# A perceiver block: places of the squares, a queue for the slots, a new layout of the preparation

## What is computed

```python
def _L0_xattn_ref(slots, P, Wq, Wk, Wv, gru_wih, gru_whh, gru_bih, gru_bhh, slot_norm_w, input_norm_w):
    ...
    Pn = rmsnorm(P, input_norm_w)
    k_proj = Pn @ Wk.T
    v_proj = Pn @ Wv.T
    for _ in range(NUM_ITERS):   # 3
        sn = rmsnorm(slots, slot_norm_w)
        q_proj = sn @ Wq.T
        scores = jnp.einsum('bkd,bmd->bkm', q_proj, k_proj) * SCALE
        attn = jax.nn.softmax(scores, axis=-2)
        attn = attn / (jnp.sum(attn, axis=-1, keepdims=True) + EPS)
        updates = jnp.einsum('bkm,bmd->bkd', attn, v_proj)
        slots = gru_cell(updates, slots, gru_wih, gru_whh, gru_bih, gru_bhh)
    return slots
...
x = x + _L0_xattn_ref(_layernorm(x, axis=-1), ctx_1024, ...)
x = x + _L0_attn_ref(...)
x = x + _L0_ffn_ref(...)
```

## Time and profile before

| | us |
|---|---|
| median of 3 runs | 1109.31 (1107.12 to 1110.37) |
| the profiled execution, its own time | 1099.15 |
| its span | 1097.4 |
| preparation, up to round 1 | 158.26 |
| rounds 1 to 12 | about 614 |

### The profile page before, as it was taken

The page is one execution under the profiler, slowest core; times in us unless marked ns, Lnnn a source line. Parts: engine busy times, 40 slices in busy tenths (PEclk is TensorE's granted clock), DMA queues, the critical chain, the costliest instruction groups (busy, mean ns, idle before and its releaser), DMA issues. The chain is left out here.

```text
span 1097.4 us, 38085 instructions
## 1 busy us (share of the span) xinstructions
PE 885.4 (81%) x17686; PEld 714.7 (65%) x17686; DVE 652.7 (59%) x1288; ACT 359.8 (33%) x651; POOL 4.6 (0%) x24
## 2 busy tenths in 40 slices
PE   3587567896988886988886899776597867999998
PEld 1444567886987886988886889776455744344443
DVE  3574537783884783874883876543624856345453
ACT  2552623333333333323333321110235623433321
POOL 0000000000000000000000000000000000000000
PEclk9788888998998998988998999897797987899999
DMA  9563970056173055253074250503123001322201
GB/s 336 220 178 72 221 147 3 4 85 174 22 113 129 3 97 162 33 105 125 5 114 144 47 128 33 117 3 117 40 46 80 21 20 54 101 94 94 99 19 38
DMA packets 159014, 99.97 MB, mean 91 GB/s; under 512 B 129740, under 2 KB 142084, under 8 KB 155788
## 3 DMA queue, kind: packets, MB, share of 16 engines
q1 hardware_dynamic: 157696, 96.42, 34.6%
q10 hardware_dynamic: 1164, 1.19, 0.3%
HBM read 60.10 MB, written 2.88 MB: 57 GB/s over the span
## 5 line engine op out<-in xcount | busy, mean ns | idle before, releaser
L881 PE MATMUL score<-qa,ctxT 128*128 128x64 f16 x3744 | 129.4, 201 | 33.2 <-DVE qa L639 18.2
L881 PEld LDWEIGHTS score<-qa,ctxT 128*128 128x128 f16 x3744 | 126.3, 104 | 35.1 <-DVE qa L639 19.2
L896 PE MATMUL score<-qa,unit 128*128 128x64 f16 (+1 forms) x2496 | 122.6, 197 | 24.5 <-issue 14.8
L896 PEld LDWEIGHTS score<-qa,unit 128*128 128x128 f16 (+1 forms) x2496 | 119.4, 101 | 19.2 <-issue 19.1
L832 PE MATMUL gate<-qa,Bt 128*128 128x64 f16 x3456 | 108.3, 195 | 20.5 <-DVE qa L680 18.2
L832 PEld LDWEIGHTS gate<-hs,whhT 128*128 128x128 f16 x3456 | 111.0, 99 | 18.4 <-issue 12.9
L896 PE MATMUL score<-scratch,unit 128*128 128x64 f16 (+1 forms) x1248 | 120.8, 197 | 2.1 <-issue 2.1
L832 PE MATMUL gate<-hs,whhT 128*128 128x64 f16 x3456 | 113.5, 195 | 10.7 <-issue 10.6
L896 PEld LDWEIGHTS score<-scratch,unit 128*128 128x128 f16 (+1 forms) x1248 | 114.6, 101 | 9.4 <-issue 9.4
L832 PEld LDWEIGHTS gate<-qa,Bt 128*128 128x128 f16 x3456 | 105.5, 99 | 22.0 <-DVE qa L680 19.4
L1624 PE MATMUL e_hid<-e_xs,e_ws 128*128 128x512 f16 x480 | 109.3, 389 | 0.0
(11 more groups left out here) (206 smaller groups left out, 1227.3 us busy)
## 6 DMA issues: line engine op xcount, KB each, us to landing
unit<-in_ctx_dram SPq DMA_DIRECT2D x24, 1024.0 KB, 8.7
ctxT<-in_L_ffn_routed_w_dram SPq DMA_DIRECT2D x24, 512.0 KB, 3.9
ctxT<-in_L_xattn_gru_wih_dram SPq DMA_DIRECT2D x3, 1024.0 KB, 16.9
ctxT<-in_L_xattn_gru_whh_dram SPq DMA_DIRECT2D x1, 3072.0 KB, 11.2
ctxT<-in_L_attn_Wqkv_dram SPq DMA_DIRECT2D x12, 256.0 KB, 8.5
ctxT<-in_L_ffn_shared_w_dram SPq DMA_DIRECT2D x6, 512.0 KB, 6.3
tail<-in_ctx_dram SPq DMA_DIRECT2D x8, 130.0 KB
unit<-in_L_xattn_Wq_dram SPq DMA_DIRECT2D x1, 1024.0 KB, 5.8
```

Source lines behind the costliest of these rows:

```text
L881: mm = pe.matmul(score[n][:, t * K:(t + 1) * K], a, q, start=(k == 0), stop=(k == 3 * DC - 1), skip_group_check=True)
L896: mm = pe.matmul(score[n][:, dc * K:(dc + 1) * K], a, q, start=first, stop=True, skip_group_check=True)
```

## The change

1. **Squares** (m = 0: of context 2k+1, all 13 in one round; m = 1: of context 2k+2): the six squares at the end of an m = 2 round and the seven at the start of the next are now in w0, w4, w5 and w2 of the m = 0 round. w0 is new on ScalarE, between exponentials(0) and attn_high(0); w5 between exponentials(1) and attn_high(1). In m = 1 rounds the first three squares go from w4 (ahead of exponentials(1)) to w5 behind it.
2. **Norms and tiles of odd contexts**: norms from w4 to w2 of m = 0; tiles from (w2 5, w3 3, next round's w1 5) to (w2 4, w3 4, w7 2, next round's w1 3). w7 is new, behind q_out(0) on VectorE and ahead of gates_out(1) on ScalarE.
3. **Slots**: load_next and store leave SyncE's queue. ScalarE issues both; the store stands right behind first_slots, the load behind w1.
4. **Preparation**: raw gru_wih lies in ctxT[0], so that gru_whh may be loaded early into ctxT[1]; the split Wq and Wk and the first slots' rows lie in whhT, the split Wv in the last third of unit[1]. The third 1 MB of context 1 is therefore loaded only after all 12 b_rows, and its squares wait for it. First slots of both lanes come from SBUF without a way over DRAM. query(1, 1) still stands ahead of query(0, 2), but the first slots of lane 1 are ready much earlier; scores(0, 1) stands behind b_row 9 in place of 7; hidden_rz(1) of step 1 moves into round 1. The small loads of norm weights and biases go to GpSimd's queue.

```diff
@@ -181,15 +181,18 @@
-wqkv_raw = unit[1][:].rearrange("p s d -> p (s d)").bitcast(F32)[:, 0:3 * DC * D].rearrange("p (j c d) -> p j c d", j=3, c=DC)
-wqkv_s = whhT[:].rearrange("p a c m -> p (a c m)").rearrange("p (j i c d) -> p j i c d", j=3, i=2, c=DC)
+in_unit1 = unit[1][:].rearrange("p s d -> p (s d)")
+raw_at = [in_unit1.bitcast(F32)[:, j * DC * D:(j + 1) * DC * D].rearrange("p (c d) -> p c d", c=DC) for j in range(3)]
+wqkv_raw = [raw_at[1], raw_at[2], raw_at[0]]
+in_whhT = whhT[:].rearrange("p a c m -> p (a c m)")
+w_qk = in_whhT[:, 0:16 * D].rearrange("p (j i c d) -> p j i c d", j=2, i=2, c=DC)
+wqkv_s = [w_qk[:, 0], w_qk[:, 1], in_unit1[:, 18 * D:].rearrange("p (i c d) -> p i c d", i=2, c=DC)]
...
-wih_raw = words(ctxT[1])[:, 0:GC * D].rearrange("p (g d) -> p g d", g=GC)
+wih_raw = words(ctxT[0])[:, 0:GC * D].rearrange("p (g d) -> p g d", g=GC)
...
-f32row = words(ctxT[0])[:, 0:2 * D].rearrange("p (i d) -> p i d", i=2)
+f32row = in_whhT[:, 16 * D:20 * D].bitcast(F32).rearrange("p (i d) -> p i d", i=2)
...
-h0_rows = [h_both[:].rearrange("p n c k -> p (n c k)"),
-           hs_both[:].rearrange("p n i c k -> p (n i c k)").bitcast(F32)]
+h0_rows = in_whhT[:, 0:4 * 2 * D].bitcast(F32).rearrange("p (t d) -> p t d", t=RT)
...
@@ -216,6 +219,10 @@
 def low_half(b, t):
...
+def first_of(b):
...
+    return h0_rows[:, b // 2].rearrange("p (c n k) -> p n c k", c=DC, n=2)[:, b % 2] if b < 2 else h_next[:]
 def result(b):
...
@@ -263,46 +273,34 @@
 def squares_in(r, place):
...
-    if m == 1:
-        spans = {"w4": (0, 3), "w2": (3, 8), "w3": (8, MT)}
-        b = 2 * k + 2
-    elif m == 2:
-        spans = {"w3": (0, 6)}
-        b = 2 * k + 3
-    else:
-        spans = {"w1": (6, MT)}
-        b = 2 * k + 1
-    return (b, *spans.get(place, (0, 0))) if b < B else (b, 0, 0)
+    spans = ({"w0": (0, 4), "w4": (4, 8), "w5": (8, 11), "w2": (11, MT)}, {"w5": (0, 3), "w2": (3, 9), "w3": (9, MT)}, {})[m]
+    b = 2 * k + 1 + m
+    return (b, *spans.get(place, (0, 0))) if 1 < b < B else (b, 0, 0)
 def tiles_in(r, place):
...
-    if m == 2:
-        spans = {"w1": (0, 4), "w4": (4, 6), "w2": (6, 10), "w3": (10, MT)}
-        b = 2 * k + 2
-    elif m == 0:
-        spans = {"w2": (0, 5), "w3": (5, 8)}
-        b = 2 * k + 1
-    else:
-        spans = {"w1": (8, MT)}
-        b = 2 * k + 1
+    spans = ({"w2": (0, 4), "w3": (4, 8), "w7": (8, 10)}, {"w1": (10, MT)},
+             {"w1": (0, 4), "w4": (4, 6), "w2": (6, 10), "w3": (10, MT)})[m]
+    b = 2 * k + (1, 1, 2)[m]
...
 def norms_in(r, place):
...
-    b = {(2, "w1"): 2 * k + 2, (0, "w4"): 2 * k + 1}.get((m, place), B)
+    b = {(2, "w1"): 2 * k + 2, (0, "w2"): 2 * k + 1}.get((m, place), B)
...
 def _(sp):
-    def load_context(b):
+    def load_context(b, groups=(0, 1, 2), landed=None):
...
-        for j in range(3):
+        for j in groups:
...
-            sp.dma_start(dst, n_rows[4 * P * j:4 * P * (j + 1), :].rearrange("(p t) d -> p (t d)", t=4)).then_inc(ctx_in, 16)
+            sp.dma_start(dst, n_rows[4 * P * j:4 * P * (j + 1), :].rearrange("(p t) d -> p (t d)", t=4))\
+                .then_inc(landed or ctx_in[b % 3], 16)
     def load_tail(b):
@@ -318,22 +316,11 @@
-    def load_next(b):
-        sp.wait_ge(h_first[(b - 1) % 2], (b - 1) // 2 + 1)
-        sp.wait_ge(h_lo[(b - 1) % 2], ITERS * ((b - 1) // 2) + 1)
-        sp.dma_start(h_next[:], h0_d[:, b // 2, :, b % 2, :]).then_inc(next_in, 16)
...
-    def store(b):
-        sp.wait_ge(h_new[b % 2], ITERS * (b // 2 + 1))
-        sp.dma_start(res_d[:, b // 2, :, b % 2, :], result(b)).then_inc(stored[b % 2], 16)
...
-    sp.dma_start(wqkv_raw[:, 0], dram.Wq.rearrange("(c p) d -> p c d", p=P)).then_inc(wqk_in, 16)
-    sp.dma_start(wqkv_raw[:, 1], dram.Wk.rearrange("(c p) d -> p c d", p=P)).then_inc(wqk_in, 16)
+    sp.dma_start(wqkv_raw[0], dram.Wq.rearrange("(c p) d -> p c d", p=P)).then_inc(wqk_in, 16)
+    sp.dma_start(wqkv_raw[1], dram.Wk.rearrange("(c p) d -> p c d", p=P)).then_inc(wqk_in, 16)
...
-    for at, src in ((0, dram.slot_norm_w), (DC, dram.input_norm_w)):
-        sp.dma_start(vec_rows[at:at + DC, :], src.rearrange("(c p) -> c p", p=P)).then_inc(small_in, 16)
...
-    sp.dma_start(wqkv_raw[:, 2], dram.Wv.rearrange("(c p) d -> p c d", p=P)).then_inc(wv_in, 16)
+    sp.dma_start(wqkv_raw[2], dram.Wv.rearrange("(c p) d -> p c d", p=P)).then_inc(wv_in, 16)
     def load_wih(g):
@@ -341,40 +328,35 @@
...
-    bih, bhh = (b.rearrange("(c p) -> c p", p=P) for b in (dram.gru_bih, dram.gru_bhh))
-    for half in range(2):
-        at = 32 * half
-        for dst, src in ((0, bih[0:2 * DC]), (2 * DC, bhh[0:2 * DC]), (4 * DC, bhh[2 * DC:GC]), (5 * DC, bih[2 * DC:GC])):
-            sp.dma_start(bias_rows[at + dst:at + dst + src.shape[0], :], src).then_inc(bias_in, 16)
...
-    sp.wait_ge(qkv_split, 3)
-    load_context(1)
...
-    sp.wait_ge(turned, GC)
...
+    sp.wait_ge(qkv_split, 3)
+    load_context(1, (0, 1))
...
+    sp.wait_ge(turned, GC)
...
-    load_next(1)
...
-    for g, (first, end, highs, lows, folds) in enumerate(((0, 16, 9, 7, DC), (16, 2 * GC, GC, GC, NF))):
-        sp.wait_ge(folded, folds)
+    for g, (first, end, highs, lows) in enumerate(((0, 16, 9, 7), (16, 2 * GC, GC, GC))):
+        if g == 0:
+            sp.wait_ge(h0_stored, 16)
+            sp.wait_ge(h_lo[1], 1)
...
+    sp.wait_ge(folded, NF)
+    load_context(1, (2,), late_in)
...
     for g in range(2):
...
-    load_next(2)
...
@@ -443,11 +430,7 @@
     def x_out(t):
...
-        if t >= 2:
-            act.wait_ge(h0_stored[t % 2], 16 * (t // 2))
-        act.copy(h0_rows[t % 2], x_bank(t)).then_inc(h0_ready, 1)
-        act.wait_ge(h0_ready, t + 1)
-        act.dma_start(h0_d[:, t].rearrange("p c n k -> p (c n k)"), h0_rows[t % 2]).then_inc(h0_stored[t % 2], 16)
+        act.copy(h0_rows[:, t], x_bank(t)).then_inc(h0_ready, 1)
     def whh_high(a, b):
...
@@ -481,9 +466,19 @@
     def first_slots(b):
-        act.wait_ge(next_in, 16 * (b + 1))
-        slots_out(b % 2, h_next[:])
-        act.copy(h[b % 2], h_next[:]).then_inc(h_first[b % 2], 1)
+        if b >= 2:
+            act.wait_ge(next_in, 16 * (b - 1))
+        slots_out(b % 2, first_of(b))
+        act.copy(h[b % 2], first_of(b)).then_inc(h_first[b % 2], 1)
...
+    def load_next(b):
+        n = (b - 1) % 2
+        if b > 2:
+            act.wait_ge(h_lo[n], ITERS * ((b - 1) // 2) + 1)
+        act.dma_start(h_next[:], h0_d[:, b // 2, :, b % 2, :]).then_inc(next_in, 16)
...
+    def store(b):
+        act.dma_start(res_d[:, b // 2, :, b % 2, :], result(b)).then_inc(stored[b % 2], 16)
     def exponentials(n, step):
@@ -506,26 +501,35 @@
-            first_slots(2 * (step // ITERS) + n)
+            b = 2 * (step // ITERS) + n
+            first_slots(b)
+            if b - 2 < 6:
+                store(b - 2)
     def place(r, name):
+        squared(*squares_in(r, name))
...
-        squared(*squares_in(r, name))
     def one_round(r):
...
+        k, m = divmod(r, 3)
...
+        if k >= 1 and m < 2 and 2 * k + 1 + m < B:
+            load_next(2 * k + 1 + m)
...
+            place(r, "w0")
...
+        place(r, "w5")
...
+        place(r, "w7")
...
@@ -537,33 +541,36 @@
+    squared(0, 0, 4)
+    for t in range(4, 8):
+        turned_block(t)
+        squared(0, t, t + 1)
...
-    for n in range(2):
-        act.wait_ge(h0_stored[n], 16 * RT // 2)
-    act.dma_start(h_next[:], h0_d[:, 0, :, 0, :]).then_inc(next_in, 16)
-    for t in range(4, GC):
+    first_slots(0)
+    first_slots(1)
+    for t in range(8, GC):
...
-        squared(0, 2 * (t - 4), min(2 * (t - 3), MT))
-        if t == 7:
-            first_slots(0)
+        squared(0, t, t + 1)
+    squared(0, MT - 1, MT)
+    act.wait_ge(h0_ready, RT)
+    act.dma_start(h0_d.rearrange("p t c n k -> p (t c n k)"), h0_rows.rearrange("p t d -> p (t d)")).then_inc(h0_stored, 16)
...
     for i in range(GC):
...
-        if i == 8:
+        if i == 10:
...
-        if i == 9:
-            attn_high(0, 1)
+    act.wait_ge(h0_stored, 16)
+    load_next(2)
+    attn_high(0, 1)
...
-    high_tiles(1, 0, 7)
+    high_tiles(1, 0, 5)
...
-    high_tiles(1, 7, MT)
+    high_tiles(1, 5, MT)
...
-    act.wait_ge(h_hi[0], 2)
-    first_slots(1)
     for r in range(1, ROUNDS):
...
@@ -622,7 +629,7 @@
     def slots_low(n, event):
...
-        src = h[n] if (event - 1) % ITERS else h_next[:]
+        src = h[n] if (event - 1) % ITERS else first_of(2 * ((event - 1) // ITERS) + n)
...
@@ -735,21 +743,23 @@
-    dve.wait_ge(small_in, 48)
+    dve.wait_ge(small_in, 16)
...
+    dve.wait_ge(x_in, 16)
+    for t in range(2):
+        st(dve.bn_stats(e.stats[:, t], xr[:, t]))
...
-    dve.wait_ge(x_in, 16)
-    for t in range(RT):
+    for t in range(2, RT):
...
-    a_row(2)
...
+    a_row(2)
+    normalise(dve, st, xr, xr, e.mv, ln_small, xn_ready)
...
-    normalise(dve, st, xr, xr, e.mv, ln_small, xn_ready)
-    for t in range(4):
+    for t in range(8):
...
@@ -757,9 +767,10 @@
-    for t in range(4, GC):
```

(30 more changed lines are left out.)

36 lines of the change are left out of this document (23 added, 13 removed).

## The result

The changed kernel took 1067.2 us (median of 4 runs, 1059.5 to 1070.0) against 1109.7 us for the kernel before: a ratio of 0.961, 95% interval 0.955 to 0.967. That is some 42 us faster where 28 were forecast. Its profiled execution took 1069.95 us with a span of 1068.2, so between the two profiled executions lie only 29 us.

A forecast was written before the change was run, and what follows sets the result against it. TensorE, with VectorE nearly as full, bounds the rounds; both idle behind ScalarE's waits for context loads. Gains 13.9 (m = 0) + 7 (m = 1) + 7.3 (preparation) = 28.2 us, from 1109.3 to 1081; range 1060 to 1100.

The forecast's parts named there:

- The squares in m = 0 rounds: Rounds 3, 6, 9: ScalarE's wait for the context load goes; 54.4 us a round, gain 13.9 us in three.
- My 5 us for stalls and half clock: In m = 0 rounds, ahead of scores(1): 5 us added for unreleased stalls and half clock, from 3.0 to 5.9.
- under 10: Expected sign: ScalarE's wait at the squares for a context's landing falls from 74.3 to under 10 us.
- The m = 1 rounds: Rounds 4, 7, 10: the store wait goes and fewer tiles stand in w1; gain 7.4 us, taken as 7.
- VectorE's wait for the store: In m = 1 rounds: earlier ScalarE issue removes it; 4.6 us gained in round 4, 1.6 in round 7.
- 3 x 0.4 for the tiles: In m = 1 rounds: w1 tiles fall to three, saving 1.5 us; w7 and store issue cost 1.1; 0.4 a round.
- the first rival: More is freed: m = 0 rounds fall to 50.0 us, m = 1 scores(1) run at full clock; 1063 us, chance 0.15.
- Slots by ScalarE: Six stores and six loads issued by ScalarE at 0.37 us each, 4.4 us; at most 1.1 counted, in the rounding.
- both rivals with a late issue: ScalarE's issue waits for SyncE's transpose in hand (1098 us, chance 0.25) or its whole row (1124, chance 0.09).
- The preparation: Up to round 1: 1.5 us from earlier norms(1) and 5.8 around query(1, 1); sum 7.3 us.
- The place of scores(0, 1): Preparation: behind b_row 9 its transposes have nearly landed, so gru_whh's are issued at about 98.5; TensorE's 6.28 us wait goes.
- hidden_rz(1) is free in round 1: Moved from the preparation, its 3.0 us land in round 1's 6.12 us hole before scores(1, 1), at no cost.

The follow-up runs named there:

- the slots' queue alone: Kernel before with only the rounds' store and load_next of slots issued by ScalarE: 1107.7 us, ratio 0.9998.
- the rounds alone: Kernel before with the change's squares, norms, tiles and ScalarE issue of slots, but the old preparation: 1077.1 us, ratio 0.972.
- the kernel with the squares alone: Kernel before with only the new places of squares and norms; tiles, slots' queue and preparation old: 1089.5 us, ratio 0.986.
- the run of the preparation alone: Changed kernel with squares, norms, tiles and slots' issue as in the kernel before, keeping the new preparation: 1099.4 us, ratio 0.992.
- the last version: Changed kernel with hidden_rz(1) back in preparation, context 1's third part loaded before gru_whh transposes, m = 1 squares from w5 to w2: 1056.4 us, ratio 0.956.

## Why the prediction was right in sign and 14 us short

**The squares in m = 0 rounds: right, a little small.** The chain was seen step by step: the squares in w0 waited for nothing, scores(1) began 17.0 us into round 3 (my terms gave 18.9), from there to the end it took 36.3 us (35.6), and the rounds took 53.3, 54.0 and 53.3 (forecast 54.4). 16.6 us in place of 13.9. My 5 us for stalls and half clock was the generous term. ScalarE's 74.3 us of waits fell to 12.5, not to under 10: 5.7 in the preparation, 2.75 and 4.05 at the squares in w5 of rounds 4 and 7, which I had taken as hidden.

**The m = 1 rounds: the term that was mis-sized.** I forecast 7 us; the profile shows 14.6. My sum had two parts, 6.2 for VectorE's wait for the store and 3 x 0.4 for the tiles. With squares and slots moved and the old tiles, m = 1 rounds gained 7.9 us (142.5), close to the 6.2. But the cause was not what I wrote: the slots' queue alone gained 0.8. The four traces above show two waits side by side, and I had let the squares' move from w4 to w5 count for nothing, because I had read ScalarE's wait there (9.78 us in round 4) only where it was longest, in m = 0. That the change moves both made the size nearly right, by luck.

The larger error is the tiles, 0.4 us a round in my sum. Against the run with the old tiles they are worth 6.8 us in the three rounds (142.6 and 135.8), and between the run of squares and slots together and the rounds alone 9.0 (142.5 and 133.5). I had counted VectorE's time for two tiles, and had seen that the last transposes begin 2 us earlier, but used that only for the load behind them. The path goes through the transposes: scores(1) starts 1.2 us earlier, meets its data, and runs in 4.79 us where I left it at 6.27, or where it waits 2.7 us for the transposes as in the run with the old tiles. I had the clock's part of it in the first rival (3 x 1.56 us) and gave that 0.15; its other half, m = 0 rounds of 50 us, did not come. The time, 1067, lies between the forecast and that rival (1063), and inside the range of 1060 to 1100.

**Slots by ScalarE: right.** Each issue cost 0.37 us, also beside SyncE's transposes, which rules out both rivals with a late issue. The Trainium skill ("Perfetto Trace Analysis", section "DMA Instruction — HWDGE (DVE, Sync)") draws a lock wait for the shared descriptor block; no issue here shows one. Two things moved. One is the time of the issue. Before, SyncE reached the store of round 4 19.5 us into the round, behind the transposes and the load:

```profile
330.99 0.39 SPq L328 DMA_DIRECT2D res_scratch<-scratch  x1
```

ScalarE issues it 3.6 us into the round (302.51 above), and VectorE needs it landed at 18.9. The other is the time to landing. The page's DMA issues, us to landing last, in the kernel with the squares alone:

```profile
res_scratch<-scratch SPq DMA_DIRECT2D x6, 128.0 KB, 9.3
```

and in the changed kernel:

```profile
res_scratch<-scratch ACTq DMA_DIRECT2D x6, 128.0 KB, 3.1
```

By the Trainium skill's "Trainium Kernel Development and Optimization", section "Key Constraints", issuing from several engines concurrently only saves issue time. The rows here show more: the same 128 KB took 6.2 us less from issue to landing once it no longer stood behind three 1 MB loads in a queue. Together the two were worth 8 to 9 us, given that nothing else held the round. No run parts them, but at 9.3 us to landing a store issued 3.6 us into the round would still be there by 13, so the earlier issue alone should do here (an estimate).

**The preparation: right order of causes, too small by 3.** The transposes of gru_whh were issued at 96.1 (I said 98.5), norms(1) ran at 120.1 (121 to 124) and behind a square that had waited for a DMA, as forecast. The gain was 10.3 us by the profile in place of 7.3; 8.5 by the run of the preparation alone. The place of scores(0, 1), one step in my sum, is worth 11 when put back by itself. That hidden_rz(1) is free in round 1 was right. That its leaving helped the preparation was not shown: put back, it fills the hole ahead of query(0, 2), and nothing is lost.

**m = 2 rounds: not explained.** They took 157.8 and 159.5 us in both profiles of the changed kernel, but 152.9, 151.4 and 152.1 in the rounds alone, with hidden_rz(1) put back, and in the last version, against 151.3 before. The other runs lie between, up to 156.6 with the slots' queue alone, which leaves squares and tiles of these rounds as they were; so a part of it is spread between executions. Round 2 took 53.0 us at a clock of 0.90, with two pauses of 1.7 and 2.1 us that nothing in the trace releases; with hidden_rz(1) put back it has the same two pauses and took 49.7 at 1.00. No edit of mine tells the cause.

**The median.** To subtract from the median was right: the code behind round 12 is the same, and took 356.4 us in the profile of before, 361.4 in that of after, and from 355.2 to 362.4 in all the others. So the 29 us between the two profiled executions understate the gain by about 5 there, and the near match with my 28.2 is an accident of that and of the m = 2 rounds.

## What to carry to other kernels

When two engines wait side by side for two different landings ahead of the same step, either wait alone can be worth nothing and the two together much; so before pricing a removed wait, look at what the partner engine is waiting for at that moment, and test parts both by taking them out of the new kernel and by putting them into the old one. Work that moves away from a place is worth more than its own time if a transfer starts behind it: follow the transfer to the instruction that needs it, as I did not for the tiles. On an engine that works in order, side work that needs a transfer is put behind the chain's own instruction, not ahead of it. A small transfer that an engine waits for is issued as soon as its data is there, from a queue in which nothing large stands ahead of it. A hole in front of TensorE's critical matmuls can be filled with work that can stand anywhere; here that left the time of the whole unchanged (1064.0 and 1066.2 us) and cost nothing.

## What the runs showed of the hardware

- A 128 KB store took 9.3 us from issue to landing behind 3 MB of loads in SyncE's queue, 3.1 us from ScalarE's. An issue on ScalarE during SyncE's transposes took 0.37 to 0.38 us.
- A hole of 6.9 us ahead of query(0, 2) came with eight fp32 matmuls of 1.97 us, and a granted clock of 0.78 from 115 us to round 1; in the last version, with 96 matmuls in the hole and a shorter wait ahead of inputs(0, 1), 1.08 us and 0.93. I had not expected a third of a 9 us gain (9.2, of which the earlier norms(1) explains 6.2) to be clock.
- The same 156 matmuls of scores(1) took 4.79 us in round 4 of the changed kernel and 6.27 before, behind a pause of 1.4 us in hidden_rz(1) that nothing in the trace releases.
- The same unchanged code behind round 12 varied from 355 to 362 us between profiled executions, more than several of the effects asked about; only the repeated timings could tell them.
